# Gaussian layer's scatter sum: from one f32 product a tile half to three exact bf16 parts, with the working values in PSUM

## The reference, cut to what matters

```python
diff = edge_vectors[:, None, :] - mu[None, :, :]
gauss = jnp.exp(-0.5 * jnp.sum(diff * diff / (EPS + sigma[None] ** 2), axis=-1))
xj = x[src] @ g
msg = jnp.sum(xj.reshape(e, k, cout) * gauss[:, :, None], axis=1)
summed = jax.ops.segment_sum(msg, dst, num_segments=n)
```

## Time and profile before

| what | us |
|---|---|
| median of 3 runs | 6453.58 (6439.67 to 6467.0) |
| the profiled execution, its own time | 6460.42 |
| its span (first to last instruction) | 6458.6 |
| of it, `stage_messages` from its first gather to its last product | 4007.1 to 5095.4 |

### The profile page before, as it was taken

How to read it: one execution, slowest core, us unless ns; L and a number is a source line. 1 busy time by engine, 2 the same in 40 slices (tenths; PEclk the granted TensorE clock), 3 DMA queues, 4 the chain that set the end, 5 groups by cost and what they waited for, 6 DMA issues and landing times. The chain is left out here.

```text
span 6458.6 us, 112027 instructions
## 1 busy us (share of the span) xinstructions
PE 4758.0 (74%) x38171; PEld 3579.6 (55%) x38171; DVE 4337.5 (67%) x11010; ACT 1867.2 (29%) x3181; POOL 4196.4 (65%) x4245
## 2 busy tenths in 40 slices
PE   5444444493668988888885755999999678888885
PEld 4444444363656766666664343555555366666664
DVE  7665565366888877777773222777777477788875
ACT  0212111254884444444442000000000033333332
POOL 1777777406946777777772533777777377777773
PEclk9999999987999999989887877999999889999998
DMA  4222222014442222222223946111111211111110
GB/s 69 87 74 79 81 74 71 18 34 118 169 164 49 58 59 57 58 55 57 58 55 101 325 142 189 38 38 37 37 37 37 37 19 22 22 22 22 22 22 16
DMA packets 387137, 441.07 MB, mean 68 GB/s; under 512 B 244355, under 2 KB 310736, under 8 KB 386397
## 3 DMA queue, kind: packets, MB, share of 16 engines
q1 hardware_dynamic: 202041, 290.11, 14.3%
q0 software_dynamic: 128224, 124.94, 11.5%
q10 hardware_dynamic: 56528, 21.19, 1.6%
HBM read 354.14 MB, written 82.34 MB: 68 GB/s over the span
## 5 line engine op out<-in xcount | busy, mean ns | idle before, releaser
L886 POOL DMA_INDIRECT ar_far<-att_table,ar_rec x1184 | 1210.4, 1022 | 422.8 <-issue 352.6
L1726 POOL DMA_INDIRECT p_far<-table,p_rec x888 | 866.2, 975 | 417.3 <-issue 262.2
L2564 PE MATMUL g_l_ps_sum<-g_l_row,g_l_of 128*128 128x392 f32 x3224 | 1064.5, 493 | 19.4 <-DVE g_l_of L2515 19.4
L2486 POOL DMA_INDIRECT g_l_got<-table,g_l_index x806 | 812.6, 1008 | 245.5 <-issue 227.8
L550 POOL DMA_INDIRECT rec_r<-so_r_rec,so_r_place x806 | 788.1, 978 | 245.5 <-issue 245.2
L2564 PEld LDWEIGHTS g_l_ps_sum<-g_l_row,g_l_of 128*128 128x128 f32 x3224 | 613.9, 190 | 470.5 <-DVE g_l_of L2515 20.5
L1500 PE MATMUL at_bank<-p_spread,p_basis 64*125 64x256 f32 x4736 | 624.1, 410 | 99.1 <-ACT p_outer L1562 99.1
L505 PE MATMUL so_r_look<-so_r_table,so_r_lo_t 128*128 128x26 f32 x1612 | 424.9, 434 | 313.2 <-DVE so_r_table L447 313.2
L2498 DVE TENSOR_SCALAR g_l_row<-g_l_iota,edge_row 128x784 f32<-128x784 f32 x806 | 500.4, 694 | 230.9 <-PE g_l_ps_sum L2564 230.8
L1500 PEld LDWEIGHTS at_bank<-p_spread,p_basis 64*125 64x125 f32 x4736 | 525.4, 196 | 179.3 <-ACT p_outer L1562 122.8
L1562 ACT COPY p_outer<-at_bank 125x512 f32<-125x512 f32 x1184 | 592.2, 715 | 101.2 <-PE at_bank L1500 100.6
(11 more groups left out here) (493 smaller groups left out, 6946.6 us busy)
## 6 DMA issues: line engine op xcount, KB each, us to landing
adjacent<-ad_by_chunk SPq DMA_DIRECT2D x74, 800.0 KB, 3.3
so_r_row<-pad_src SPq DMA_DIRECT2D x62, 832.0 KB, 6.1
g_l_counts<-adjacent SPq DMA_DIRECT2D x60, 800.0 KB, 7.1
g_l1d_counts<-adjacent SPq DMA_DIRECT2D x59, 800.0 KB, 6.8
so_r_low<-pad_lo_src SPq DMA_DIRECT2D x62, 416.0 KB, 4.6
ar_far<-att_table,ar_rec POOLq DMA_INDIRECT x1184
p_far<-table,p_rec POOLq DMA_INDIRECT x888
rec_r<-so_r_rec,so_r_place POOLq DMA_INDIRECT x806
```

The source lines that it names most:

```text
L886: pool.indirect_dma_start(out=self.far[q][:, t, :], out_offset=None, in_=self.g.att_table[:, :], in_offset=bass.IndirectOffsetOnAxis(ap=se ...
L1726: pool.indirect_dma_start(out=sl.far[b][:, t, :], out_offset=None, in_=table[:, :], in_offset=bass.IndirectOffsetOnAxis(ap=sl.rec[b][:, t, ...
L2486: pool.indirect_dma_start(out=got[b][:, j, :], out_offset=None, in_=table[:, :], in_offset=bass.IndirectOffsetOnAxis(ap=index[b][:, j:j + ...
L2564: last = nc.tensor.matmul(ps_sum[k][:], of4[b][:, j, :, :].rearrange("p k f -> p (k f)"), row1[b][:, j, k * COLS:(k + 1) * COLS], start=Fa ...
```

## The change

Values and one-hots become bf16, and three bf16 parts of each value stand for the f32 value:

- `of4`, the spread values, is now one tile in PSUM (four banks, no longer two copies in SBUF), and `mixed`, the sum over kernels, lies in a bank of `ps_turn[0]`, which is not used until the end.
- Each step's `of4` is cut into three bf16 parts in SBUF. ACT casts `of4` to part 0, DVE subtracts part 0 from `of4` in place, ACT casts the rest to part 1, and DVE subtracts part 1 and writes part 2. The steps are tied by the semaphores `cut`, `rest` and `parted`.
- `row1` is bf16. DVE makes 9 of the 13 row one-hots of a step, 4 while ACT casts the first time and 5 while ACT makes one-hots and casts the second time. ACT makes the other 4, each from two activations: Abs(row - iota) into `apart`, then Relu(1 - apart), with the semaphores `aparts` and `hots`.
- The multiplication by the Gaussians goes in five pieces of at most three tiles, the first addition in two halves, the spreading in pieces that begin at bank borders.
- DVE's work on the values of a step now comes ahead of its one-hots; the index tile of the step after the next is written right after the spreading.
- PE waits for `parted` and `hots` and does six products a tile, three parts by two halves, in bf16.

```diff
--- before.py
+++ after.py
@@ -2463,13 +2463,19 @@
         zero = sb("zero", [P, P])
         index = [sb(f"index{b}", [P, HB], I32) for b in two]
         got = [sb(f"got{b}", [P, HB, 3 * F]) for b in two]
-        mixed = sb("mixed", [P, HB, F])
-        of4 = [sb(f"of4{b}", [P, HB, 4, F]) for b in two]
-        row1 = [sb(f"row1{b}", [P, HB, TALL]) for b in two]
+
+        of4 = ps("of4", [P, HB, 4, F])
+
+        part = [[sb(f"part{b}{k}", [P, HB, 4, F], BF16) for k in range(3)] for b in two]
+        row1 = [sb(f"row1{b}", [P, HB, TALL], BF16) for b in two]
+        apart = sb("apart", [P, TALL])
+        by_dve = HB - 4
         sums, turned_rows = sb("sums", [P, WIDE]), sb("turned_rows", [P, chunks, P])
         ps_sum = [ps(f"ps_sum{k}", [P, COLS]) for k in two]
         ps_turn = [ps(f"ps_turn{k}", [P, 4, P]) for k in two]
+        mixed = ps_turn[0][:].rearrange("p q c -> p (q c)")[:, 0:HB * F].rearrange("p (t f) -> p t f", f=F)
         gathered = [rows_sem(nc, f"{name}_gathered{b}") for b in two]
+        cut, rest, parted, hots, aparts = (sem(n) for n in ("cut", "rest", "parted", "hots", "aparts"))
         iotas, steps, indexed, mixes, ready, summed, all_in, copied, turned, out, stored, taken = (
             sem(n) for n in ("iotas", "steps", "indexed", "mixes", "ready", "summed", "all_in", "copied", "turned", "out", "stored", "taken"))
         with nc.Block() as block:
@@ -2493,28 +2499,55 @@
                 def index_of(step, b):
                     nc.vector.tensor_copy(index[b][:], g.edge_src[:, bass.ds(step * HB, HB)]).then_inc(indexed, 1)
 
-                def one_hots(step, b):
-                    for j in range(HB):
+                def one_hots(step, b, js):
+                    for j in js:
                         last = nc.vector.tensor_scalar(row1[b][:, j, :], iota[:], g.edge_row[:, bass.ds(step * HB + j, 1)], None, ALU.is_equal)
                     ch.put(last)
 
+                pieces = ((0, 4), (4, 8), (8, HB))
+
                 def mix(step, b, turn):
                     cols = bass.ds(step * HB, HB)
 
                     dve.wait_ge(gathered[b], turn * (16 * HB) + 16 * HB)
                     rows3 = got[b][:].rearrange("p t (k f) -> p t k f", k=3)
-                    for at, end in ((0, 5), (5, 9), (9, HB)):
+                    for at in range(0, HB, 3):
+                        end = min(at + 3, HB)
                         here = bass.ds(step * HB + at, end - at)
                         ch.put(nc.vector.tensor_mul(rows3[:, at:end], rows3[:, at:end],
                                                     g.edge_gauss[:, here, :].unsqueeze(3).to_broadcast([P, end - at, 3, F])))
                     ch.wait()
-                    ch.step(nc.vector.tensor_add(mixed[:], rows3[:, :, 0, :], rows3[:, :, 1, :]))
-                    ch.step(nc.vector.tensor_add(mixed[:], mixed[:], rows3[:, :, 2, :]))
-                    for at, end in ((0, 5), (5, 9), (9, HB)):
+                    for half in (slice(0, 6), slice(6, HB)):
+                        ch.put(nc.vector.tensor_add(mixed[:, half], rows3[:, half, 0, :], rows3[:, half, 1, :]))
+                    ch.wait()
+                    ch.step(nc.vector.tensor_add(mixed, mixed, rows3[:, :, 2, :]))
+                    for at, end in pieces:
                         b4, here = [P, end - at, 4, F], bass.ds(step * HB + at, end - at)
-                        last = nc.vector.tensor_mul(of4[b][:, at:end, :, :], mixed[:, at:end, :].unsqueeze(2).to_broadcast(b4),
+                        last = nc.vector.tensor_mul(of4[:, at:end, :, :], mixed[:, at:end, :].unsqueeze(2).to_broadcast(b4),
                                                     g.edge_of4[:, here, :].unsqueeze(3).to_broadcast(b4))
                     last.then_inc(ready, 1)
+
+                def one(step, b, turn, first=False, last_pair=False):
+                    if not first:
+
+                        dve.wait_ge(summed, step - 1)
+                        dve.wait_ge(parted, step)
+                    mix(step, b, turn)
+                    if not last_pair:
+                        index_of(step + 2, b)
+                    one_hots(step, b, range(by_dve // 2))
+
+                    dve.wait_ge(cut, step * 2 + 1)
+                    for at, end in pieces:
+                        here = nc.vector.tensor_sub(of4[:, at:end], of4[:, at:end], part[b][0][:, at:end])
+                    here.then_inc(rest, 1)
+                    one_hots(step, b, range(by_dve // 2, by_dve))
+                    ch.wait()
+
+                    dve.wait_ge(cut, step * 2 + 2)
+                    for at, end in pieces:
+                        here = nc.vector.tensor_sub(part[b][2][:, at:end], of4[:, at:end], part[b][1][:, at:end])
+                    here.then_inc(parted, 1)
 
                 for b in two:
                     index_of(b, b)
@@ -2524,24 +2557,16 @@
                 dve.wait_ge(iotas, 1)
                 ch.step(nc.vector.tensor_copy(iota[:], iota_i[:]))
                 dve.sem_inc(mixes, 1)
-                for b in two:
-                    one_hots(b, b)
-                    mix(b, b, 0)
-                    index_of(b + 2, b)
+                one(0, 0, 0, first=True)
+                dve.wait_ge(parted, 1)
+                one(1, 1, 0, first=True)
                 with dve.Fori(1, half - 1) as i:
                     ch.restart()
                     for b in two:
-                        n = i * 2 + b
-
-                        dve.wait_ge(summed, n - 1)
-                        one_hots(n, b)
-                        mix(n, b, i)
-                        index_of(n + 2, b)
+                        one(i * 2 + b, b, i)
                 ch.restart()
                 for b in two:
-                    dve.wait_ge(summed, STEPS - 3 + b)
-                    one_hots(STEPS - 2 + b, b)
-                    mix(STEPS - 2 + b, b, half - 1)
+                    one(STEPS - 2 + b, b, half - 1, last_pair=True)
                 full, left = divmod(WIDE, P)
                 dve.wait_ge(turned, 1)
                 nc.vector.tensor_copy(turned_rows[:, 0:4, :], ps_turn[0][:]).then_inc(out, 1)
@@ -2558,11 +2583,13 @@
                 with pe.Fori(0, half) as i:
                     for b in two:
 
-                        pe.wait_ge(ready, i * 2 + (b + 1))
+                        pe.wait_ge(parted, i * 2 + (b + 1))
+                        pe.wait_ge(hots, i * 8 + (4 * b + 4))
                         for j in range(HB):
-                            for k in two:
-                                last = nc.tensor.matmul(ps_sum[k][:], of4[b][:, j, :, :].rearrange("p k f -> p (k f)"),
-                                                        row1[b][:, j, k * COLS:(k + 1) * COLS], start=False, stop=False)
+                            for of in part[b]:
+                                for k in two:
+                                    last = nc.tensor.matmul(ps_sum[k][:], of[:, j, :, :].rearrange("p k f -> p (k f)"),
+                                                            row1[b][:, j, k * COLS:(k + 1) * COLS], start=False, stop=False)
                         last.then_inc(summed, 1)
                 for k in two:
                     nc.tensor.matmul(ps_sum[k][:], zero[:], iota[:, 0:COLS], start=False, stop=True).then_inc(all_in, 1)
@@ -2575,6 +2602,31 @@
 
             @block.scalar
             def _(act):
+                def one_hots(step, b, js):
+                    for j in js:
+
+                        act.wait_ge(hots, step * 4 + (j - by_dve))
+                        nc.scalar.activation(apart[:], iota[:], ACT.Abs, bias=g.edge_row[:, bass.ds(step * HB + j, 1)], scale=-1.0).then_inc(aparts, 1)
+                        act.wait_ge(aparts, step * 4 + (j - by_dve + 1))
+                        nc.scalar.activation(row1[b][:, j, :], apart[:], ACT.Relu, bias=g.ones[:, 0:1], scale=-1.0).then_inc(hots, 1)
+
+                def one(step, b, first=False):
+                    if not first:
+
+                        act.wait_ge(summed, step - 1)
+                    one_hots(step, b, range(by_dve, by_dve + 2))
+                    act.wait_ge(ready, step + 1)
+                    nc.scalar.copy(part[b][0][:], of4[:]).then_inc(cut, 1)
+                    one_hots(step, b, range(by_dve + 2, HB))
+                    act.wait_ge(rest, step + 1)
+                    nc.scalar.copy(part[b][1][:], of4[:]).then_inc(cut, 1)
+
+                act.wait_ge(mixes, 1)
+                for b in two:
+                    one(b, b, first=True)
+                with act.Fori(1, half) as i:
+                    for b in two:
+                        one(i * 2 + b, b)
                 for k in two:
                     act.wait_ge(all_in, k + 1)
                     nc.scalar.copy(sums[:, k * COLS:(k + 1) * COLS], ps_sum[k][:]).then_inc(copied, 1)
```

## The result

Five runs of each kernel: 6428.1 us in the median (6411.6 to 6434.7) against 6458.4 (6439.7 to 6467.0). The ratio is 0.9946 (95% interval 0.9928 to 0.9965), a gain of 30 us. The profiled execution took 6411.6 us, with a span of 6409.3: 49 us under the one of before. Of these, 36.4 us lie in the changed stage, which took 1050.8 us from its first gather (4006.25) to its closing products (5057.01), before 1087.2. The other 12.9 us lie in stages that the change doesn't touch, most of it in the last spline stage. I take them for the difference between one execution and another: the five of the kernel before lie 27 us apart, and the profiled one of the changed kernel is the fastest of its five.

What follows compares the result with a forecast made beforehand. PE set the step at 17.1 us, with POOL's gathers close behind. At 16.64 us for 62 steps the gathers save 26.5 us, the tail adds 0.4: 26 less than 6453.6 gives 6428 us, range 6400 to 6478.

Steps and rivals of the forecast that it cites:

- The size of PE's gain: PE's products: 26 f32 products, 17.2 us a step, become 78 bf16 ones at 12.9, gaining 4.3 that turns into waiting.
- three steps: Steps before the change, at the start and once later, where 13 gathers took 16.69, 16.79 and 16.44 us.
- The mean of 16.64: Mean of three steps thought unpaced by PE, taken as POOL's new step and the floor for PE's gain.
- the stretching of the gathers: Gather time over the usual 0.944 us; forecast between 0 (16.2 us a step) and 0.9 (17.1), taken at 16.64.
- PSUM's effect: Skill's rule: DVE instructions with at most one SBUF input leave POOL's gathers alone; the sum used the unpaced steps instead.
- Rival B: POOL's gathers run at their floor as stretches vanish: 51 us less, 6403, or 6414 with half gone; chance 0.24.
- Rival E: Gathers stretched as before by one-hot entries and the mix, 0.26 us each: no real gain, 6452; chance 0.14.
- The low end: DVE writes to PSUM at the SBUF price, 1.04 ns a value; the high end was two passes a value.
- Rival C: DVE becomes the bound because PSUM writes cost two passes: 20 us more (6474) or 153 more (6607); chance 0.09.
- The margin between ACT's second cast and DVE's arrival: ACT's casts and activations end 7.5 us after spreading, DVE comes after 7.9, so they fit by 0.4 us.
- The tail: Behind the last gather: landing 1.6 us, DVE 15.2, PE 12.9, together 29.7, 0.4 more than before.
- Rival D: PE's clock falls to 0.50: short spells covered by its rest; if it stayed there, 550 us more; chance 0.03.

## Why the prediction was right, point by point

**The bound that takes over.** The prediction said that the gathers would set the step and that what PE gains would turn into a wait. PE's group shows it, and one gather less gave 78 us where PE's 192 us less came with 36. The size of PE's gain was off: 14.1 us a step (872.1 / 62) and not 12.9, because of the clock, and so a wait of 2.4 us a step and not 3.7.

**What held POOL before.** The prediction speaks of three steps in which POOL was "not held to PE's pace". The rows show that POOL was held by no wait in any step: the index tile written at 4508.52 to 4508.82 is the one for the gathers that begin at 4518.19, 9.4 us later, and in the whole stage the tile is there 9.2 us or more ahead from the second step on. Still POOL kept PE's pace. Two windows of the kernel before over the same 41 steps, POOL's gathers and PE's products:

```profile
4312.79:5014.55 701.76, 539.34 (x533) 1.00 0.19 37
4312.79:5014.55 701.76, 701.76 (x2133) 1.00 0.19 37
```

That is 17.12 us a step for the 13 gathers, with 0.88 us of stretches, and 17.12 for PE's 52 records, without a gap. DVE's instructions start when PE releases them and stretch the gathers that they meet; that this feedback brings the two to one pace is my reading, and no run isolates it. The mean of 16.64 was thus a mean over steps in which DVE and POOL stood differently to each other, not over steps set free.

**The step.** Predicted 16.64 us, measured 16.47. The mis-sized term is the stretching of the gathers, 0.4 a step, taken from those three steps; it came out at 0.23. The prediction held PSUM's effect to be a rule beside the sum and took the old order's stretches. Sorted by DVE's instruction, the 51.7 us of stretches before were 18.9 under the spreading, 16.7 under the one-hots and 15.9 under the first addition. Now they are 14.4 us: none under the spreading, 9.8 and 3.9 under the other two. So half of the 37 us less lies where an operand moved to PSUM. The other half lies under instructions that still read SBUF alone. What makes it smaller was not isolated: they run at other moments, the first addition is cut in two and writes PSUM, and the one-hots are bf16. Had all values stayed in SBUF in the new order, its subtractions would have stretched gathers as well; the estimate from those runs is 0.3 to 0.5 us a step, 20 to 30 us, most of the measured gain. Rival B, the floor of 16.25, came within reach: somewhat under half of the way there from 16.64 was made good. Rival E counted three stretched gathers a step at 0.26 us each, which is what the kernel before has (2.9 at 0.29). The changed kernel has 1.1 a step at 0.20.

**PSUM as a target.** Taken at the price of SBUF, with twice that as the other end. The groups by shape of the changed kernel, of ACT and DVE:

```profile
L2609 ACT ACTIVATE g_l_apart<-g_l_iota,edge_row 128x784 f32<-128x784 f32 x248 | 235.3, 949 | 74.6 <-PE g_l_ps_sum L2591 47.9 <-DVEq L2559 10.3
...
L2619 ACT CAST g_l_part<-g_l_of 128x1664 bf16<-128x1664 f32 x62 | 95.9, 1546 | 315.9 <-DVE g_l_of L2526 315.9
...
L2526 DVE TENSOR_TENSOR g_l_of<-g_l_ps_turn,edge_of 128x512 f32<-128x512 f32 x124 | 80.4, 695 | 8.8
...
L2542 DVE TENSOR_TENSOR g_l_of<-g_l_of,g_l_part 128x512 f32<-128x512 f32 x124 | 79.2, 681 | 0.0
...
L2523 DVE TENSOR_TENSOR g_l_ps_turn<-g_l_ps_turn,g_l_got 128x416 f32<-128x416 f32 x62 | 37.2, 599 | 2.1
```

512 values take 0.695 us when spread from PSUM into PSUM and 0.681 when subtracted in place, against 0.684 in SBUF; 416 values take 0.599 against 0.59. The low end was right to 2%. Rival C is out.

**DVE and ACT.** DVE was put at 15.2 us a step and takes 14.8 in the median (14.9 in the step shown). The one-hots are as quick as put, 0.62 and 0.63 us; the index tile, 0.15 us from start to start and not 0.30, and the two subtractions, 0.1 us less each, make the difference. ACT's activation was put at 0.95 and takes 0.949, its cast at 1.65 and takes 1.55. The margin between ACT's second cast and DVE's arrival, put at 0.4 us, is 0.57 in the median and 0.10 at the least. In the last step, where no gather holds DVE's one-hots up, DVE waits 0.26 us for it, as the timeline of the tail shows.

```profile
5025.82 0.94 POOL L2492 DMA_INDIRECT g_l_got<-table,g_l_index  x1 [0.31 <-issue]
...
5028.43 1.73 DVE L2517 TENSOR_TENSOR g_l_got<-g_l_got,edge_gauss 128x288 f32<-128x288 f32 x5 [1.72 <-DMA g_l_got<-table,g_l_index]
...
5040.58 2.02 DVE L2549 TENSOR_TENSOR g_l_part<-g_l_of,g_l_part 128x512 bf16<-128x512 f32 x3 [0.26 <-ACT g_l_part L2622]
...
5042.73 14.45 PE L2591 MATMUL g_l_ps_sum<-g_l_row,g_l_part 128*128 128x392 bf16 x78 [2.77 <-DVE g_l_part L2549]
...
5057.01 1.48 PE L2595 MATMUL g_l_ps_sum<-g_l_iota,g_l_zero 128*128 128x392 f32 x4
```

**The tail.** From the last gather's end (5026.76) to the closing products (5057.01) it takes 30.2 us, predicted 29.7. The landing is 1.7 us, DVE's part 14.2 instead of 15.2, PE's 14.45 instead of 12.9, at a mean granted clock of 0.90 behind its rest.

**The clock.** Rival D had it that spells at 0.50 would be covered by PE's rest. Three PE groups in the timeline:

```profile
4500.36 15.95 PE L2591 MATMUL g_l_ps_sum<-g_l_row,g_l_part 128*128 128x392 bf16 x78 [3.37 <-DVE g_l_part L2549]
4516.81 13.11 PE L2591 MATMUL g_l_ps_sum<-g_l_row,g_l_part 128*128 128x392 bf16 x78 [0.49 <-DVE g_l_part L2549]
4533.31 1.02 PE L2591 MATMUL g_l_ps_sum<-g_l_row,g_l_part 128*128 128x392 bf16 x3 [3.40 <-DVE g_l_part L2549]
```

After 3.37 us of rest the 78 products take 15.95 us; the window of this step had a clock of 0.83. After 0.49 us of rest they take 13.11 us, at 1.00. The two mostly alternate: a slowed PE step leaves a short rest, and the next is not slowed. Of the 61 steps after the first, 28 are slowed (14.4 to 16.1 us), all behind rests of 1.95 to 3.4 us; 27 behind rests of 0.4 to 1.8 us are not, and neither are 6 behind rests of 3.0 to 3.4 us. None reaches 16.47, so it costs the steps nothing, and some 1.5 us once in the tail. The mild form of rival D came true, at no cost to the steps, as the prediction had it.

**The sum.** Predicted 26 us less; the stage gave 36 in the profile, the median 30. The step's 0.17 us of error, times 62, is the 10 us between 26 and 36. That the median of 6428.1 meets the forecast of 6428 to the microsecond is luck: the kernel before came out 5 us higher in the median of five runs than in that of three, and the medians show 4 us more gain than the sum, the stage 10.

## What to carry to other kernels

When two engines fill a stage, here to 17.17 and 17.07 us a step, relieving one frees the step only as far as the other's own pace allows. Find that pace in the durations of its instructions, and not only in its waits: POOL had no wait before the change either, and the whole gain is that its gathers became shorter. Before relieving an engine, count what it does to the queue that comes next: here the sequence that relieves PE loads DVE to 14.8 us a step, 1.7 under the new bound. It also brings new DVE instructions, which would have lengthened the gathers by an estimated 20 to 30 us had their values stayed in SBUF. When a run's chip disturbs the steps, a term taken from it has to be tested against a run of the same kernel on an undisturbed chip: 12 gathers had 0.24 us of stretches a step on one and up to 0.77 on the other. And a change that puts many short instructions in place of few long ones should be tried on more than one chip.

## What was not expected of the hardware

Two of three further chips run the kernel before 41 to 42% slower (9.1 to 9.2 ms). In the variants of the changed kernel profiled there, the instructions have the same length (78 products in 13.11 us, three spreadings in 2.03), but PE's products come one each 2.1 to 2.9 us for some 17 us, as shown for 12 gathers. With 78 products a step this begins in 30 of 31 turns of PE's loop at nearly the same place, 36 to 46 products after the start of the turn. Why is open. Kernels with six products a tile took 1.3 to 1.9% longer than the one before on these chips, those with values in SBUF and all one-hots on DVE, and the one with 12 gathers 0.8% longer; the one with 26 products a step in place of 52 f32 records took 1.1 to 2.0% less. The changed kernel itself was not run there, so whether it loses on them is open, though a kernel with its work less one gather did.

A DVE one-hot of 784 values takes 0.55 us once POOL has finished (five in 2.77 us in the tail), and 0.62 beside the gathers: the two fall into step, two one-hots to a gather of 1.25 us. PE's granted clock can alternate from step to step without any change in the work, by the rest that the step before left; with 12 gathers it did so behind rests of some 2.1 us (78 products in 14.75 us). And an engine can keep another's pace through the length of its instructions alone, without one wait, as POOL did before the change.
